# First and second slots staggered per sequence and per expert, features as 128 + 64 on array halves, and the combination joined to the experts

## The chip, the cores and the metric

The kernel runs on one core of a Trainium2 chip. The metric is the device time of one execution in microseconds (us). The core has TensorE (PE; its weight loads are shown as PEld), VectorE (DVE), ScalarE (ACT), GpSimd (POOL) and SyncE (SP, which here only issues transfers). Work on different engines is ordered by semaphores alone. TensorE writes its results to PSUM, which has eight banks of 2 KB in each of 128 partitions.

## What is computed

Eight sequences of 256 tokens with 192 features pass through a token mixer, an attention with 12 heads, and a mixture of experts with two levels of soft slots. The change lies in the last of these. Cut to what matters:

```python
# GROUP = 64 tokens, E1 = 8 outer experts, S1 = 16 slots each, E2 = 4 inner experts each
xn = l2norm(x) * scale * gamma_in ; xg = xn.reshape(b, G, 64, d)         # 32 groups in all
logits1 = einsum('bGgd,esd->bGges', xg, phi)                              # 64 tokens x 128 slots
disp1 = softmax(logits1, axis=2); comb1 = softmax(logits1 over the 128 slots)
slots = einsum('bGgd,bGges->bGesd', xg, disp1)
yn = l2norm(slots) * scale * gamma2
means = yn.reshape(b, G, E1, 4, 4, d).mean(axis=4)
se2 = l2norm(einsum('bGkmd,kdf->bGkmf', means, w_slot2)) * scale          # 192 x 768 weights per k
logits2 = einsum('bGksd,bGkemd->bGksem', yn, se2)
disp2, comb2 = softmax over s, softmax over (e, m)
slots2 = einsum('bGksd,bGksem->bGkemd', yn, disp2)
act = v * gelu(gate), (v, gate) = split(slots2 @ w1 + b1)                 # 32 inner experts
o = act @ w2 + b2
out = einsum(comb1, einsum(o, comb2))                                     # added to the residual h
```

## The kernel before

Everything is float32 outside the attention. A stage is one function with a block of instructions for every engine; between two stages all engines meet. The stages that matter here, in order:

- `fold_weights` (L93) forms, besides the folded weights, the transposed slot table `g.phi_t`, 96 features by two halves by 128 slots.
- `first_slots` (L1181) works on the eight sequences in two rounds of `WIDE` = 4 (a register loop). Within a round every step is done for all four sequences before the next one begins: row statistics, normalized rows `x`, four transposes (L1234), logits to slots and to tokens with the 192 features as 96 + 96 (L1242, L1246), maxima (L1388, L1391), exponentials (L1304, L1308), transposes of both softmax tables (L1253, L1259), the slots (L1267), their squares and norms (L1333, L1415), the means of four slots (L1274, a 128 x 32 stationary matrix) and their transposes (L1280). DVE norms the rows; POOL only clears memory. The dispatch table `disp` has zeros in the rows of the other group, so that each slot product contracts over 128 rows.
- `second_slots` (L1477) makes `se2` for each outer expert k, two buffers in turn in a register loop: a copy of the means (L1596), four products of 384 columns (L1529, 96 + 96 features), squares and root on ACT (L1560 to L1567), scaling on DVE (L1581), eight transposes (L1540) and two copies out, one on DVE and one on ACT (L1590, L1573). SP fetches the weights `w_slot2` of k + 2 when those of k are used (`load_slot2`, L1464).
- `second_dispatch` (L1603) is written out for the eight sequences. PE's order in one iteration n is logits of n (L1649), dispatch turned of n - 1 (L1666), `yn` turned of n + 1 (L1639), logits turned of n (L1658), expert inputs of n - 1 (L1687), weights of n (L1675). The last waits for a product on POOL (L1827), which waits for the row sums of ACT's exponentials (L1724).
- `experts` (L1831) is written out for the 32 inner experts. Its hidden layer already has the features as 128 + 64: whole products (L1882) and then products over 64 rows, alternately in the lower and the upper half of the array (L1887). Each expert's 128 rows are copied from PSUM (L1939), stored to DRAM by ACT's queue (L1919), and once per four experts gathered back into `g.yn` by POOL (L1949), which turns rows of experts into rows of groups.
- `combine` (L1954) adds the bias `b2` to the gathered rows on DVE and POOL (L1980, L1994), copies the mixing weights (L2002), multiplies (L2014), adds the residual (L1984) and stores (L2025).

## Time and profile before

| | us |
|---|---|
| median of three runs | 701.97 |
| lowest and highest | 698.33, 703.11 |
| the profiled execution | 702.88 |
| its span, first to last instruction | 701.1 |
| `first_slots` | 348.5 to 422.7 of the span |
| `second_slots` | 422.7 to 459.9 |
| `second_dispatch` | 459.9 to 532.3 |
| `experts`, its arithmetic | 532.3 to 673.9 |
| gather of the last rows, meeting of the engines | 673.9 to 683.1 |
| `combine` | 683.1 to 701.1 |

The profile is one execution. PE is busy 82% of the span, PEld 67%, DVE 55%, ACT 43%, POOL 10%. Its page shows the granted clock of TensorE in tenths of full speed (2.4 GHz) for 40 slices; the clock has two levels, 1.2 and 2.4 GHz, so that a value of 0.74 means a mixture. A product in float32 has two records in the trace, a transpose has one.

### The profile page before, as it was taken

How to read it: one execution, taken by the hardware profiler on the slowest of the kernel's cores; microseconds unless marked ns; L12 is line 12 of the kernel's file. 1: busy time of each engine (PE TensorE's matmuls, PEld its weight loads, DVE VectorE, ACT ScalarE, POOL GpSimd, SP SyncE). 2: the span in 40 equal slices, each digit the busy share in tenths (PEclk: the TensorE clock that was granted, in tenths of full speed). 3: DMA queues.
4: the chain of work that ended last, by engine and by line, in shares of the span. 5: the costliest groups of instructions: out<-in, count | busy, mean ns of one | idle time of the engine just before them, and what ended most of it. 6: DMA issues, size and time to landing. Idle time of an engine off the chain costs nothing. (4 is left out here: it accounts for less than half of the span.)

```text
span 701.1 us, 12206 instructions
## 1 busy us (share of the span) xinstructions
PE 574.3 (82%) x4294; PEld 469.3 (67%) x4294; DVE 383.4 (55%) x960; ACT 299.5 (43%) x855; POOL 69.8 (10%) x90
## 2 busy tenths in 40 slices
PE   6497997387989989897566877969998999999935
PEld 5386786253666666664365654559987999999934
DVE  2117636658899999986257452435652333333315
ACT  1123432243566566654157775735563222222211
POOL 5682000001000000000000000000000000000004
PEclk9799898665999999999577779968999999999986
DMA  9300000000000000000090003300005999999412
GB/s 320 94 0 2 1 0 1 0 0 1 1 2 2 0 0 0 2 1 1 7 332 0 1 0 93 110 0 1 3 1 216 377 313 322 315 320 284 69 40 91
DMA packets 19656, 58.25 MB, mean 83 GB/s; under 512 B 2627, under 2 KB 9397, under 8 KB 19478
## 3 DMA queue, kind: packets, MB, share of 16 engines
q1 hardware_dynamic: 13366, 47.84, 19.4%
q0 software_dynamic: 1056, 4.73, 3.8%
q10 hardware_dynamic: 5184, 5.02, 2.3%
q8 instruction: 30, 0.49, 0.3%
q14 instruction: 20, 0.16, 0.1%
HBM read 52.86 MB, written 4.72 MB: 82 GB/s over the span
## 5 line engine op out<-in xcount | busy, mean ns | idle before, releaser
L1930 DVE SCALAR_TENSOR_TENSOR ex_act_t<-banks,b_sb,ex_gelu 128x128 f32<-128x128 f32 x128 | 36.1, 345 | 95.6 <-ACT ex_gelu L1913 95.6
L1913 ACT ACTIVATE ex_gelu<-banks,b_sb 128x128 f32<-128x128 f32 x128 | 36.6, 369 | 100.7 <-PE banks L1887 100.7
L1882 PE MATMUL banks<-slots_t,w 128*128 128x128 f32 x512 | 62.5, 275 | 1.0 <-PEq L1606 1.0
L1882 PEld LDWEIGHTS banks<-slots_t,w 128*128 128x128 f32 x512 | 61.2, 192 | 1.4 <-issue 1.3
L1074 DVE TENSOR_REDUCE att_max<-banks 128x4 f32<-128x1024 f32 x48 | 58.6, 1221 | 2.2 <-PE banks L736 1.3
L924 ACT ACTIVATE att_prob<-banks 128x1024 f32<-128x1024 f32 x48 | 49.1, 1023 | 16.6 <-PE banks L759 16.6
L1900 PE MATMUL banks<-w,ex_act_t 128*128 128x192 f32 x256 | 50.2, 339 | 0.6 <-DVE ex_act_t L1930 0.6
L1900 PEld LDWEIGHTS banks<-w,ex_act_t 128*128 128x128 f32 x256 | 40.7, 189 | 4.6 <-DVE ex_act_t L1930 0.9
L1887 PE MATMUL banks<-slots_t,w 64*128 64x128 f32 x512 | 37.2, 285 | 0.0
L736 PE MATMUL banks<-k_t,q_t 96*128 96x256 bf16 x192 | 31.0, 287 | 4.3 <-DVE att_max L1074 4.1
L774 PE MATMUL banks<-att_prob,val 128*32 128x256 f32 x384 | 28.6, 419 | 7.0 <-ACT att_prob L924 6.8
L759 PE MATMUL banks<-q_t,k_t 104*128 104x256 bf16 x192 | 30.7, 284 | 4.0 <-ACT att_prob L924 3.0
L1887 PEld LDWEIGHTS banks<-slots_t,w 64*128 64x128 f32 x512 | 31.1, 187 | 3.9
L709 PE MATMUL banks<-ident_b,att_stack 128*96 128x128 bf16 x384 | 28.4, 231 | 5.2 <-DVE att_stack L1041 2.4
L679 PE MATMUL banks<-qkv_t_sb,xt 96*128 96x384 f32 (+1 forms) x64 | 29.1, 591 | 3.3 <-ACT xt L870 3.3
L709 PEld LDWEIGHTS banks<-ident_b,att_stack 128*96 128x96 bf16 x384 | 26.2, 132 | 7.4 <-DVE q_t L1045 3.5
L899 ACT COPY k_t<-banks 96x1024 bf16<-96x1024 bf16 x24 | 24.1, 1006 | 15.3 <-PE banks L709 15.3
L1166 POOL TENSOR_TENSOR att_qk<-att_qk,qk_weight 128x192 f32<-128x192 f32 x16 | 9.2, 599 | 211.5 <-DVE att_qk L1009 211.5
L1529 PE MATMUL banks<-w_slot,ss_mean_k 96*128 96x384 f32 x64 | 24.0, 524 | 2.9 <-DVE ss_mean_k L1596 2.3
L736 PEld LDWEIGHTS banks<-k_t,q_t 96*128 96x128 bf16 x192 | 15.9, 101 | 13.2 <-DVE att_max L1074 8.6
L759 PEld LDWEIGHTS banks<-q_t,k_t 104*128 104x128 bf16 x192 | 18.1, 100 | 9.8 <-ACT att_prob L924 4.5
L774 PEld LDWEIGHTS banks<-att_prob,val 128*32 128x32 f32 x384 | 10.5, 115 | 19.0 <-ACT att_prob L924 10.6
(231 smaller groups left out, 1171.1 us busy)
## 6 DMA issues: line engine op xcount, KB each, us to landing
w<-in_w SPq DMA_DIRECT2D x32, 768.0 KB, 7.4
w<-in_w2e SPq DMA_DIRECT2D x32, 384.0 KB, 8.1
w_slot<-in_w_slot SPq DMA_DIRECT2D x8, 576.0 KB, 4.5
rows_scratch<-ex_rows ACTq DMA_DIRECT2D x32, 96.0 KB, 6.4
yn_all<-rows_scratch POOLq DMA_DIRECT2D x8, 384.0 KB, 7.2
out<-co_final SPq DMA_DIRECT2D x8, 192.0 KB, 1.9
wk_t<-in_wk_t ACTq DMA_DIRECT2D x1, 579.0 KB, 5.1
wq_t<-in_wq_t SPq DMA_DIRECT2D x1, 579.0 KB, 5.5
```

The costliest lines, as they stand in the source:

```text
L679: last = nc.tensor.matmul(g.ps[banks[1 + t]][:, 0:2 * DIM], x_t[s][0:k, c, t * P:(t + 1) * P], g.t["qkv_t"][0:k, c, 0:2 * DIM], start=(c = ...
L709: last = nc.tensor.transpose(bank[0:KS, h * SEQ + t * P:h * SEQ + (t + 1) * P], stack[:, row, :, :].rearrange("p a b -> p (a b)"), ident_b ...
L736: last = nc.tensor.matmul(g.ps[hh][:, t * SEQ:(t + 1) * SEQ], q_t[s][0:KS, h, t * P:(t + 1) * P], k_t[s][0:KS, h, :], start=True, stop=True)
L759: last = nc.tensor.matmul(g.ps[2 + hh][:, m * SEQ:(m + 1) * SEQ], k_t[s][:, h, m * P:(m + 1) * P], q_t[s][:, h, :], start=True, stop=True)
L774: last = nc.tensor.matmul(bank[32 * j:32 * j + 32, (q % 2) * SEQ:(q % 2 + 1) * SEQ], val[s][:, m, QH * q + j, :], prob[j // 2][:, j % 2, m ...
L924: nc.scalar.activation(prob[u][:, :, :, :].rearrange("p a b n -> p (a b n)"), flat(2, 4), ACT.Exp).then_inc(S["exped"], 1)
L1074: nc.vector.tensor_reduce(neg_max[:, 2 * u:2 * u + 2, :].rearrange("p a b -> p (a b)"), flat(0, 2).rearrange("p (g n) -> p g n", n=SEQ), A ...
L1882: nc.tensor.matmul(bank[:, j * P:(j + 1) * P], g.w1[e][:, first + j * P:first + (j + 1) * P], x[:, 0, :], start=(j == 0), stop=False, skip ...
L1887: last = nc.tensor.matmul(bank[:, j * P:(j + 1) * P], g.w1[e][part, 2 * HID + j * P:2 * HID + (j + 1) * P], x[part, 1, :], start=False, st ...
L1900: last = nc.tensor.matmul(out_bank(n)[:, 0:DIM], act_t[n % 2][:, j * P:(j + 1) * P], g.w2[e][:, j, :], start=(j == 0), stop=(j == HB - 1))
L1913: nc.scalar.activation(gelu[n % 2][:, j * P:(j + 1) * P], gate_bank(n)[:, j * P:(j + 1) * P], ACT.Gelu_apprx_tanh, bias=g.t["b1"][:, n, HB ...
L1930: nc.vector.scalar_tensor_tensor(out=act_t[n % 2][:, j * P:(j + 1) * P], in0=value_bank(n)[:, j * P:(j + 1) * P], scalar=g.t["b1"][:, n, j ...
```

## The change

The arithmetic results stay the same. Four parts:

1. `first_slots` is written out without a loop and staggered: in iteration n each engine works on different steps of sequences n - 3 to n + 1. The features are 128 + 64; sequence tile t has its 64 in the lower (t = 0) or upper (t = 1) half of the partitions. Slots contract over the 64 rows of their group. Normed rows of sequences 1 to 7 and the scaling of the combination table move from DVE to POOL. Slots are normed straight into `g.yn`. The epsilon of the norm comes from a column of 1e-3 beside `x`, so products have 193 columns and two small DVE operations and the accumulation of `disp_sum` fall away. One bank (TURN) takes the turned `x`, dispatch and combination in turn; one pair (SLOTS) takes all slots.
2. `second_slots` is staggered per outer expert, features 128 + 64, three pairs of banks and three weight buffers; the means need no copy; all copies out are on DVE, four per expert.
3. `second_dispatch` reads that layout: six transposes instead of eight, logits as four whole and four half products, expert inputs of the last 64 features alternately in the two column halves. Turned logits and turned dispatch share a bank.
4. `combine` is gone. The experts' stage ends with 32 products of the bias `b2` and 32 products of the gathered rows, accumulated in the eight banks; DVE adds each bank to the residual and SP stores it. The rows of the last four experts go straight from `rows` to `g.yn` by four transfers each, two from SP's queue and two from ACT's; POOL gathers the first seven groups only.

The core of the diff (where an engine's loop calls its steps, the calls stand in order on one or two lines, without their bounds on n and k):

```diff
 def first_slots(nc, g):
+            def logits(n):
+                pe.wait_ge(S["kept"], n + 1)
+                for part in range(2):
+                    for to_slots in (True, False):
+                        for t in range(TPS):
+                            rows, c = chunks(t)[part]     # (0:128, 2t), then (0:64 or 64:128, 1)
+                            last = nc.tensor.matmul(g.ps[LOGITS(n)[t]][:, first:first + P], lhs, rhs,
+                                                    start=(part == 0 and to_slots), stop=(part == 1), ...)
+            def make_slots(n):
+                pe.wait_ge(S["disp_kept"], n + 1)
+                pe.wait_ge(S["slots_normed"], GPS * n)
+                for t in range(TPS):
+                    for half in range(2):
+                        rows = slice(GROUP * half, GROUP * (half + 1))
+                        last = nc.tensor.matmul(g.ps[SLOTS[half]][:, AND_ONE(t)], disp[n % 2][rows, t, :],
+                                                x[n % NX][rows, AND_ONE(t)], start=True, stop=True)
+            # PE
+            for n in range(BATCH + 4):
+                turn_disp(n - 1); logits(n); turn(n + 1); turn_means(n - 3)
+                turn_comb(n - 1); make_slots(n - 1); make_means(n - 2)
+            # ACT
+                squares(n - 2); root_slots(n - 2); keep_mean_rows(n - 3); keep(n + 1); disp_exp(n); comb_exp(n)
+            # DVE
+                keep_disp(n - 1); maxima(n); norm_slots(n - 2); keep_comb(n - 1); keep_means(n - 3)
+                invert(n); row_stats(n + 4)
+            # POOL
+                scale_comb(n); make_x(n + 3)
...
 def second_slots(nc, g):
+            # PE
+            for k in range(E1 + 2):
+                make(k); turn(k - 2)
+            # DVE: norm(k), then keep(k - 1) with four copies of 256 columns. ACT: root(k)
...
 def second_dispatch(nc, g):
-        TURN, LOGITS, TURNED, DISP, WEIGHTS, INPUTS = (0, 1), 2, 3, 4, 5, (6, 7)
+        TURN, LOGITS, SHARED, WEIGHTS, INPUTS = (0, 1), (2, 3), 4, 5, (6, 7)
             def turn_logits(n):
                 pe.wait_ge(S["masked"], n + 1)
-                pe.wait_ge(S["col_exped"], GPS * n)
+                pe.wait_ge(S["disp_kept"], n)
...
 def experts(nc, g):
+            for n in by_bank:                               # (3, 7, 0, 1, 2, 4, 5, 6)
+                mix(n, lambda gr: g.t["b2"], True)
+            pe.wait_ge(gathered, 16 * (E1 - 1))
+            pe.wait_ge(moved, 16 * MEAN * E2)
+            for n in by_bank:
+                mix(n, lambda gr: g.yn[:, n * GPS + gr, :], False).then_inc(S["mixed"], 1)
+        # SP: two transfers of each of the last four experts' rows, then one store per bank
+        # ACT: the other two transfers; DVE: g.h += bank, as mixed counts up
-            for k in range(E1):
+            for k in range(E1 - 1):
...
-def combine(nc, g):
```

## Rows read from the trace of the kernel before

**Rows 1.** Stages: stretch; length, busy PE, PEld, DVE, ACT, POOL, clock, DMA, GB/s.

```profile
348.50:422.70 74.20, 50.87 (x304) 41.64 (x304) 43.01 (x161) 50.24 (x220) 2.46 (x8) 0.74 0.23 80
422.70:459.90 37.20, 31.64 (x128) 19.35 (x128) 14.20 (x24) 21.87 (x88) 0.00 (x0) 0.93 0.34 96
459.90:532.30 72.40, 64.67 (x512) 60.34 (x512) 37.59 (x72) 36.81 (x152) 4.91 (x8) 0.89 0.00 1
532.30:673.90 141.60, 140.45 (x1280) 132.16 (x1280) 44.73 (x160) 37.89 (x129) 3.60 (x7) 1.00 0.86 276
683.10:701.10 18.00, 10.15 (x64) 7.71 (x64) 10.72 (x12) 2.95 (x8) 8.65 (x4) 0.69 0.25 88
```

**Rows 2.** Waits in the first slots: total us, times, longest.

```profile
DVE fs_neg_slot L1388 <- PE banks L1246: 14.3, 8, 4.2
```

**Rows 3.** Timeline in the first slots: start, us, engine, line, what.

```profile
362.51 1.03 PE L1242 MATMUL banks<-fs_x_t,phi_t 96*128 96x256 f32 x4
364.27 1.03 PE L1242 MATMUL banks<-fs_x_t,phi_t 96*128 96x256 f32 x4
...
395.21 0.42 DVE L1388 TENSOR_REDUCE fs_neg_slot<-banks 128x4 f32<-128x256 f32 x1 [4.07 <-PE banks L1246]
...
404.90 6.40 PE L1267 MATMUL banks<-fs_x,fs_disp 128*128 128x192 f32 x32
...
411.47 1.39 DVE L1415 SCALAR_TENSOR_TENSOR fs_yn<-banks,fs_slot_fac,gamma_sb 128x192 f32<-128x192 f32 x4
412.92 0.53 PE L1274 MATMUL banks<-fs_yn,average 128*32 128x192 f32 x8 [1.61 <-DVE fs_yn L1415]
413.47 1.39 DVE L1415 SCALAR_TENSOR_TENSOR fs_yn<-banks,fs_slot_fac,gamma_sb 128x192 f32<-128x192 f32 x4
```

**Rows 4.** Timeline in the second slots.

```profile
443.54 2.75 PE L1529 MATMUL banks<-w_slot,ss_mean_k 96*128 96x384 f32 x8
445.24 0.96 DVE L1581 TENSOR_TENSOR ss_se<-banks,ss_factor 128x768 f32<-128x768 f32 x1 [2.14 <-ACT ss_factor L1567]
446.26 1.08 PE L1540 MATMUL banks<-ident,ss_se 128*96 128x128 f32 x8
447.29 2.85 PE L1529 MATMUL banks<-w_slot,ss_mean_k 96*128 96x384 f32 x8
```

**Rows 5.** Timeline of the second dispatch, and one group of its lines.

```profile
489.44 1.10 PE L1675 MATMUL banks<-comb_t,sd_comb 128*128 128x64 f32 x8 [0.29 <-POOL comb_t L1827]
490.38 2.00 PE L1649 MATMUL banks<-se_t,w_slot 96*128 96x128 f32 x16
496.82 1.10 PE L1675 MATMUL banks<-comb_t,sd_comb 128*128 128x64 f32 x8 [0.28 <-POOL comb_t L1827]
L1687 PE MATMUL banks<-sd_disp,yn_all 128*64 128x128 f32 x16 | 1.6, 279 | 0.0
```

**Rows 6.** Timeline in the experts: whole products, then half products.

```profile
552.96 1.92 PEld L1882 LDWEIGHTS banks<-slots_t,w 128*128 128x128 f32 x16
553.12 1.95 PE L1882 MATMUL banks<-slots_t,w 128*128 128x128 f32 x16
555.00 1.16 PE L1887 MATMUL banks<-slots_t,w 64*128 64x128 f32 x16
```

**Rows 7.** POOL's product with two inputs: a group of the lines.

```profile
L1994 POOL TENSOR_TENSOR co_rows<-yn_all,b_sb 128x768 f32<-128x768 f32 x4 | 8.6, 2181 | 7.0 <-POOLq L1836 6.7 <-PE banks L2014 0.3
```

**Rows 8.** Timeline of the end.

```profile
673.54 0.36 DVE L1939 COPY ex_rows<-banks 128x192 f32<-128x192 f32 x1 [1.39 <-PE banks L1900]
676.09 0.49 POOL L1949 DMA_DIRECT2D yn_all<-rows_scratch  x1 [14.50 <-DMA rows_scratch<-ex_rows]
...
693.31 4.50 PE L2014 MATMUL banks<-co_rows,co_mix 128*64 128x192 f32 x32 [3.12 <-DVE co_rows L1980]
...
697.37 1.23 DVE L1984 TENSOR_TENSOR co_final<-h,banks 128x384 f32<-128x384 f32 x2 [0.72 <-PE banks L2014]
```

**Rows 9.** A stretch of the combination at 1.2 GHz, columns as in the first group.

```profile
683.10:690.00 6.90, 5.46 (x32) 3.70 (x32) 5.01 (x5) 2.54 (x7) 6.75 (x3) 0.50 0.17 59
```

More of the change, by code:

```diff
@@ L42 @@
 BUFS = 8
+SLOT_BUFS = 3
 EARLY = 4
@@ L1347, in _, with keep @@
-            root(0)
-            with act.Fori(0, BATCH // WIDE - 1) as i:
-                body(i, more=True)
-            body(BATCH // WIDE - 1, more=False)
+                act.wait_ge(S["logged"], pair + 1)
+                nc.scalar.activation(factor[:, cols], log_v[:, cols], ACT.Exp, scale=-0.5).then_inc(S["rooted"], 1)
+            def keep(n):
+                act.wait_ge(S["turned"], n + 1)
+                if n >= 2:
+                    act.wait_ge(S["logits"], n - 1)
+                nc.scalar.copy(x_t[n % 2][:, :, :], g.ps[TURN][:, 0:3 * P].rearrange("p (c n) -> p c n", c=3)
+                               ).then_inc(S["kept"], 1)
@@ new lines, in _ @@
+            root(0)
+            keep(0)
+            root(1)
+            for n in range(BATCH + 4):
+                if 0 <= n - 2 < BATCH:
+                    squares(n - 2)
+                    root_slots(n - 2)
+                if 0 <= n - 3 < BATCH:
+                    keep_mean_rows(n - 3)
+                if n + 1 < BATCH:
+                    keep(n + 1)
+                if n < BATCH:
+                    disp_exp(n)
+                    comb_exp(n)
+                if n in (1, 3):
+                    root(2 + n // 2)
@@ new lines, in _ @@
+            for n in range(2):
+                row_stats(n)
+            make_x(0)
+            for n in range(2, 4):
+                row_stats(n)
+            for n in range(BATCH + 4):
+                if 0 <= n - 1 < BATCH:
+                    keep_disp(n - 1)
+                if n < BATCH:
+                    maxima(n)
+                if 0 <= n - 2 < BATCH:
+                    norm_slots(n - 2)
+                if 0 <= n - 1 < BATCH:
+                    keep_comb(n - 1)
+                if 0 <= n - 3 < BATCH:
+                    keep_means(n - 3)
+                if n < BATCH:
+                    invert(n)
+                if n + 4 < BATCH:
+                    row_stats(n + 4)
@@ L1577, in _, with norm @@
+                nc.scalar.activation(log_s[:, k, :], ss[:, k, :], ACT.Ln, scale=1.0 / DIM,
+                                     bias=g.eps_dim[:, :]).then_inc(S["logged"], 1)
+                act.wait_ge(S["logged"], k + 1)
+                nc.scalar.activation(factor[:, k, :], log_s[:, k, :], ACT.Exp, scale=-0.5).then_inc(S["rooted"], 1)
+            for k in range(E1):
+                root(k)
         @block.vector
         def _(dve):
-            def norm(i, s):
-                dve.wait_ge(S["rooted"][s], i + 1)
+            def norm(k):
+                dve.wait_ge(S["rooted"], k + 1)
+                if k >= 2:
+                    dve.wait_ge(S["turned"], k - 1)
@@ L1603, in second_dispatch @@
+            for k in range(E1 + 1):
+                if k < E1:
+                    norm(k)
+                if k >= 1:
+                    keep(k - 1)
 def second_dispatch(nc, g):
```

803 lines of the change are left out of this document (376 added, 427 removed).

## Prediction

> **What bounds the kernel now.** I first cut the span into its stages, since a share of busy time over the whole span says little [rows 1]. In the experts PE is busy 140.45 of 141.60 us at full clock. The change leaves their arithmetic alone, so those 141.6 us stay. In the first slots no engine is full: PE 50.9, ACT 50.2 and DVE 43.0 of 74.2 us, and the clock is 0.74. The waits say why: each step is done for four sequences while the other engines stand, for instance DVE waits 14.3 us in all for logits [rows 2]. In the second slots PE is busy 31.6 of 37.2 us, in the second dispatch 64.7 of 72.4 us, so there PE's own work counts. The timeline of the end shows a stretch without arithmetic: the last expert's rows are copied at 673.54 to 673.90, the gather is issued at 676.09, and the combination begins at 683.1 and takes 18.0 us with PE busy 10.2 [rows 1, 8]. From the last copy to the end are 27.2 us.
>
> **Prices.** A whole product of 128 columns costs 0.122 us per record (1.95 / 16). Over 64 rows in alternate array halves it costs 0.073 (1.16 / 16), a factor of 0.6 [rows 6]. A transpose costs 0.135 (1.08 / 8) [rows 4]. A change between whole and half products leaves PEld idle for 555.00 - (552.96 + 1.92) = 0.12 us, while the PE records leave no gap [rows 6]. So such a switch costs between 0 and 0.12 us; I take 0.12, as weight loads set this pace. The Trainium skill, "TensorEngine Tiling (Array Packing)", Key Properties, says that changing the tiling mode drains the engine, and gives no figure for it. By that rule the 0.12 is a drain, and by the PE records alone it would be free; what each makes of the first slots stands below, in its own bounds.
>
> **First slots.** The loop that closes from one iteration to the next runs PE, DVE, PE, because make_slots(n - 1) has to wait until norm_slots(n - 2) has read the only pair of slot banks, and DVE puts maxima(n) ahead of that norm. Its terms:
> - two transposes of the dispatch, 0.27;
> - logits, 8 whole records at 0.122 and 8 half ones at 0.073: 1.56 (now 1.76, from 362.51 to 364.27 [rows 3]);
> - two maxima of 256 columns, 2 x 0.42 = 0.84;
> - norm of four slots, 1.39 (rows of 192 columns);
> - slots, 8 half records of 193 columns: 6.40 / 32 = 0.20 whole, times 0.6 = 0.12, so 0.96;
> - means, 0.53;
> - five hand-overs between engines, as an estimate 0.3 in all (two of them, 0.04 us each: DVE's reduction starts as PE's records end);
> - four more switches, 0.5.
>
> That is 6.35 us per sequence at 2.4 GHz [rows 3, 6]. 3.3 us of it is PE work, which at 1.2 GHz nearly doubles. What clock will be granted? The stage has 0.74 now, about half its time at the lower level. The staggered PE has gaps of about 1 us and work in about 4.3 of 6.35 us, denser than now (50.9 of 74.2 includes the wait for the half clock itself). I take a quarter of the time at the lower level: 6.35 + 0.8, so 7.1. Six iterations take 43 us. The first two have no norm on the path: 3.75 each, 7.5. Ahead lie statistics, root, one normed sequence, transposes and copy, 5 us. At the end nothing overlaps: norm of 6, slots of 7, squares and root (2.0, the distance of two norms on rows 3, and 0.4 for the wait), norm, means, their copies and transposes: 10.8. The sum is 66, against 74.2: **-8**. Bounds: all at 2.4 GHz and switches free, 5.85 per iteration, gives 58 (-16); a clock of 0.74 as now and every switch paid gives 8.0 per iteration and 73 (-1). Other engines lie beside this loop. ACT has now 50.2 / 8 = 6.3 us per sequence and loses the 32 accumulator reads of the dispatch and the copy into `g.yn`, so about 5. DVE has 0.4 + 0.84 + 1.39 + 0.4 + three copies of the means 0.8 + statistics 0.9, about 5. POOL is new here. Its row is 2.18 us for 768 columns with two inputs, taken in proportion: 0.73 for the table of 256 and 1.09 + 2 x 0.55 for one normed sequence, 2.9 in all; the bounds are 0.6 times that (one input) and a fixed part that doubles it to 5.8, still under the loop [rows 7].
>
> **Second slots.** Now 447.29 - 443.54 = 3.75 us per expert [rows 4]. After: four whole records of 384 columns at 2.75 / 8 = 0.344, four half at 0.6 of it, 2.2 us; transposes 0.98; two switches 0.24: 3.4. Seven times 0.35 saves 2.4, the copy of the means ahead of the first product 0.5. But DVE now takes all copies, four of about 0.38 after the 0.96 of the scaling, and with one pair of TURN banks the last transposes wait for them: two rounds of transposes and copies (5 us) now follow one another where one and a half did, +2. Together **-1**, between -4 (switches free, tail as now) and +2.
>
> **Second dispatch.** The period is 496.82 - 489.44 = 7.38 us [rows 5]. PE gets shorter by 2 transposes (0.25), logits 1.79 to 1.56 (0.23), and the 16 records over 64 columns (1.6 us) at about 0.6 of that, 0.6. It would save 1.0 less 0.24 for two switches. But the chain logits, mask, row maximum, exponentials, reciprocal, POOL, weights is already the last to arrive (PE waits 0.28 for POOL), and it gets shorter only by the logits and by an earlier turned `yn`, 0.4 to 0.5. The shared bank makes turn_logits(n) wait for ACT's copy of the dispatch; behind it on PE stand the inputs and weights. The copy is ready about 0.15 us late, which the same chain hides. **-3.5** for eight iterations, from 0 to -7.
>
> **End.** Removed: store, gather, meeting of engines, bias additions, copies of the mixing weights. Added: 64 records of 192 columns for the bias on PE, right after the last expert. At 1.2 GHz such a record takes 5.46 / 32 = 0.17 us [rows 9]; at a mixed clock 4.50 / 32 = 0.14 [rows 8]. After the experts the clock is 1.00 [rows 1], so between 0.085 (half) and 0.14; I take 0.10. PE: 673.5 + 6.4 + 6.4 = 686.3, then as now from the last product (697.8) to the end, 3.3: 689.6, **-11.5**. Bounds: 0.085, -13.5; 0.17 throughout, -2.5. The four last transfers are issued from 673.9, two on each queue, behind nothing but each other (SP's weight loads are long done), and the bias products cover them until 679.9. Without that cover they would cost their issue and landing, some 3 us. The store now lands within 676.09 - 673.9 = 2.2 us [rows 8].
>
> **Sum.** -8 - 1 - 3.5 - 11.5 = -24. Against the profiled execution, 702.88 us (0.9 above the median), this gives 679, and 678 by the median; I state **679**.
>
> **Rivals.**
> - *A, the clock stays at 1.2 GHz in the three stages* (the other side). For it: the clock is 0.74 in the first slots now, and spreading the work leaves a gap of about 1 us in each iteration. Against: 0.93 and 0.89 in the second slots and the second dispatch, where PE also waits in every iteration [rows 1, 5]. Price: first slots 6.35 + 3.0 = 9.3 per iteration, 81 in all (+7); second slots 3.4 to about 4.9 (+8); second dispatch, PE's 6 us to 11 per iteration, 88 against 72.4, +16; end -11.5: together +20, **722**. It ends slower once more than about half of the three stages runs at the lower level. The Trainium skill, "TensorE: Matmul & The Clock Gate", Part 4: PE-mode transpose, says that transposes do not count as activity for the clock; by that rule a third of the staggered PE work would not help to hold it. Chance 0.06.
> - *B, the first slots gain nothing*: the loop is 8 us or more, because POOL's rows of `x` or the half products are dearer than taken. Time 702.9 - 16 = **687**. For it: POOL's price is taken from another operation. Chance 0.16.
> - *C, the end gains little*: the mixing products run at 0.17, or the last transfers land after the bias products. 27.2 - 2.5 of it stays: **688**. Against: 1.00 right before. Chance 0.10.
> - *D, all at 2.4 GHz and switches free*: -16 - 3 - 6 - 13.5, **664**. Chance 0.13.
> - *Forecast*, 671 to 686: 0.55.
>
> **How the numbers follow.** The range takes in D's end, B and C: 664 to 692, and leaves out A and mixtures of B and C. Over 1% (7 us, about what a measurement of this kernel can tell) faster are forecast, B, C and D but for 0.05 where B and C come together: 0.89. Within 1%: 0.05. Slower: 0.06.
>
> **What would show it.** In the profile after: the first slots in 66 us with make_slots at a distance of about 7.1 and released by DVE's norm; a clock over 0.8 there; half products at 0.6 of whole ones; second slots about 36 us; second dispatch about 69; no gap over 0.5 us on PE between the last expert and the last mixing product, and 16 us from the last copy to the end. I am wrong if PE waits for POOL in the first slots, if the clock there is under 0.7, or if the final products wait for a transfer.

## The result, and the profile after

| | before | after |
|---|---|---|
| median of the runs, us | 700.7 (698.33 to 703.11) | 672.65 (668.68 to 672.94) |
| span of the profiled execution, us | 701.1 | 671.0 |
| mean granted clock | 0.883 | 0.898 |

The ratio is 0.9586, with a 95% interval of 0.9535 to 0.9638: 4.1% faster. The forecast was 679 with a range of 664 to 692. Direction and range held. The two profiled executions differ by 29.9 us and the medians by 28, where 24 were forecast, so I look at each stage.

The same cut into stages for the kernel after, to be read beside [rows 1]. I put the borders at the end of the last attention addition, the first product of the second slots, the first transposes of the second dispatch, the first product of the experts, and the end of the last copy of rows. Columns: stretch, length, busy PE, PEld, DVE, ACT, POOL, clock, DMA share, GB/s.

```profile
347.33:410.32 62.99, 40.52 (x328) 28.24 (x329) 37.28 (x131) 33.71 (x168) 26.21 (x37) 0.85 0.27 104
410.32:446.15 35.83, 29.60 (x128) 16.48 (x129) 21.20 (x40) 14.88 (x80) 0.00 (x0) 0.83 0.25 83
446.15:514.90 68.75, 59.41 (x497) 51.86 (x497) 36.87 (x72) 36.03 (x153) 4.91 (x8) 0.88 0.00 1
514.90:655.95 141.05, 140.85 (x1286) 132.55 (x1288) 44.60 (x160) 37.84 (x129) 3.58 (x7) 1.00 0.87 276
655.95:671.00 15.05, 10.37 (x126) 9.19 (x122) 4.44 (x8) 0.00 (x0) 0.00 (x0) 0.98 0.35 115
```

With the same borders the kernel before has 74.66, 36.90, 72.42, 141.42 and 27.20 us, after 348.50 us of embedding, mixer and attention (347.33 in the kernel after). So:

| stage | before | after | change | forecast |
|---|---|---|---|---|
| first slots | 74.66 | 62.99 | -11.7 | -8 |
| second slots | 36.90 | 35.83 | -1.1 | -1 |
| second dispatch | 72.42 | 68.75 | -3.7 | -3.5 |
| experts | 141.42 | 141.05 | -0.4 | 0 |
| end | 27.20 | 15.05 | -12.15 | -11.5 |

These give -28.9. Another 1.2 lies ahead of the first slots, in code that is the same in both but for the layout of the transposed slot table. That part moves by itself: in the profiles of this study the attention ends between 347.2 and 349.9 us, whatever the kernel. I therefore compare **spans less the end of the attention**: 352.6 for before, 323.7 for after. For a kernel that was profiled twice (after, and after once more) this number is 323.67 and 323.70, where the spans differ by 2.6.

**The loop of the first slots.** One iteration in the timeline of the kernel after (start, us, engine, line, what, and in brackets the idle time ahead and what ended it). It answers [rows 3].

```profile
380.76 0.44 PE L1276 MATMUL banks<-ident,fs_disp_t 128*128 128x128 f32 x2
381.04 0.61 PE L1258 MATMUL banks<-fs_x_t,phi_t 128*128 128x128 f32 x4
381.72 0.21 ACT L1374 ACTIVATE fs_slot_fac<-fs_slot_log 128x4 f32<-128x4 f32 x1
382.35 0.39 PE L1258 MATMUL banks<-phi_t,fs_x_t 64*128 64x128 f32 x4
382.79 0.42 DVE L1412 TENSOR_REDUCE fs_neg_slot<-banks 128x4 f32<-128x256 f32 x1 [1.12 <-PE banks L1258]
383.46 1.38 DVE L1436 SCALAR_TENSOR_TENSOR yn_all<-banks,fs_slot_fac,gamma_sb 128x192 f32<-128x192 f32 x4
...
384.76 0.41 DVE L1423 COPY comb_t<-banks 128x256 f32<-128x256 f32 x1
384.99 0.93 PE L1286 MATMUL banks<-fs_x,fs_disp 64*128 64x193 f32 x8 [0.75 <-DVE yn_all L1436]
385.09 0.93 DVE L1444 COPY means_t<-banks 128x128 f32<-128x128 f32 x3
386.16 0.53 PE L1295 MATMUL banks<-yn_all,average 128*32 128x192 f32 x8 [0.25 <-DVE means_t L1444]
386.63 0.44 PE L1276 MATMUL banks<-ident,fs_disp_t 128*128 128x128 f32 x2
```

Up to the slots the chain runs as the forecast drew it: transposes, logits, DVE's maxima, DVE's norm, slots (released by that norm). From 380.76 to 386.63 one iteration takes 5.87 us. Its pieces are 1.98 + 0.05 for transposes and logits, 0.67 for the maxima, 1.38 + 0.15 for the norm, 1.17 for the slots and 0.47 for the means. The 1.17 are 0.93 of products and then a wait that the forecast did not have: the means of one sequence go to the bank from which DVE copies the turned means of the one before, and DVE comes to these three copies only behind the norm and the copy of the combination table. They end at 386.02, TensorE's slot products about 0.1 us earlier, and the means begin at 386.16. The distance of the slot products is 5.86 to 5.87 us each time from the third of them to the seventh.

And the clock, over three stretches of that stage:

```profile
347.33:360.00 12.67, 6.61 (x40) 5.39 (x40) 6.23 (x27) 3.49 (x14) 7.23 (x16) 0.64 0.92 351
360.00:400.00 40.00, 28.77 (x262) 20.43 (x259) 25.94 (x89) 27.92 (x142) 18.99 (x22) 1.00 0.13 53
400.00:410.32 10.32, 5.14 (x32) 2.42 (x31) 5.11 (x17) 2.30 (x12) 0.00 (x0) 0.54 0.01 2
```

In the loop it is 1.00, so 2.4 GHz throughout. It is low at the start, where TensorE waits for statistics and the first features, and in the drain.

Between whole and half products the weight loads leave a gap:

```profile
381.37 0.53 PEld L1258 LDWEIGHTS banks<-phi_t,fs_x_t 128*128 128x128 f32 x4
382.02 0.30 PEld L1258 LDWEIGHTS banks<-fs_x_t,phi_t 64*128 64x128 f32 x4
```

**POOL.** From the groups of lines of the stage (count, busy us, mean ns, idle before):

```profile
L1499 POOL TENSOR_SCALAR fs_centred<-h,fs_mv,fs_factor 128x192 f32<-128x192 f32 x14 | 14.0, 1009 | 5.0 <-DVE fs_x L1457 3.4 <-ACT fs_factor L1334 1.6
L1505 POOL TENSOR_TENSOR fs_x<-fs_centred,gamma_in_sb 128x384 f32<-128x384 f32 x7 | 7.0, 1003 | 0.6
```

A sequence costs 2 x 1.01 + 1.00 and 0.61 for the table, 3.6 us.

**Second slots and second dispatch.** Timeline of TensorE at their border, to be read beside [rows 4, 5]:

```profile
438.21 1.75 PE L1587 MATMUL banks<-ident,ss_se 128*128 128x128 f32 x8 [1.97 <-DVE se_t L1635]
441.92 1.94 PE L1587 MATMUL banks<-ident,ss_se 128*128 128x128 f32 x8 [1.97 <-DVE se_t L1635]
...
455.67 1.97 PE L1726 MATMUL banks<-comb_t,sd_comb 128*128 128x64 f32 x8 [2.60 <-POOL comb_t L1883]
...
465.72 1.10 PE L1726 MATMUL banks<-comb_t,sd_comb 128*128 128x64 f32 x8 [0.66 <-POOL comb_t L1883]
...
472.68 0.55 PE L1726 MATMUL banks<-comb_t,sd_comb 128*128 128x64 f32 x3 [0.36 <-POOL comb_t L1883]
```

The last two rounds of transposes run one behind the other with DVE's copies and TensorE idles 1.97 us ahead of each. The clock is at its lower level from 438.4 to 452.1 us and again from 455.5 to 462.3, and the first period of the dispatch is long: 465.72 - 455.67 = 10.05 us, where the next is 472.68 - 465.72 = 6.96. Another 9.5 us lie ahead of the first of these products.

**The end**, beside [rows 8]:

```profile
655.48 5.42 PE L1980 MATMUL banks<-b_sb,mix_t 128*64 128x192 f32 x64
655.59 0.36 DVE L2037 COPY ex_rows<-banks 128x192 f32<-128x192 f32 x1 [1.40 <-PE banks L1972]
662.66 5.42 PE L1980 MATMUL banks<-yn_all,mix_t 128*64 128x192 f32 x64 [1.76 <-DMA yn_all<-ex_rows]
663.57 5.11 DVE L2043 TENSOR_TENSOR h<-h,banks 128x384 f32<-128x384 f32 x8 [7.62 <-PE banks L1980]
```

Each mixing record takes 5.42 / 64 = 0.085 us, and there is a wait that the forecast did not have: 1.76 us for the last transfers.

### The profile page after: what moved, and what is told of

Its sections match the earlier page's. It is cut to its first block and busy times, and to the rows that moved or that the text cites. A ratio compares the mean times of both kernels' runs of the same rounds, so it can differ in the third digit from the quotient of the medians.

```text
span 671.0 us, 12001 instructions
## 1 busy us (share of the span) xinstructions
PE 558.5 (83%) x4367; PEld 447.4 (67%) x4367; DVE 377.9 (56%) x944; ACT 272.0 (41%) x787; POOL 84.4 (13%) x114
## 5 line engine op out<-in xcount | busy, mean ns | idle before, releaser
L777 PE MATMUL banks<-att_prob,val 128*32 128x256 f32 x384 | 30.0, 437 | 7.0 <-ACT att_prob L927 6.8
L739 PEld LDWEIGHTS banks<-k_t,q_t 96*128 96x128 bf16 x192 | 15.9, 101 | 13.5 <-DVE att_max L1077 8.6
L1099 DVE COPY q_t<-banks 8x1024 bf16<-8x1024 bf16 x24 | 16.7, 697 | 12.0 <-PE banks L749 11.3
```

The source lines that it names most:

```text
L739: last = nc.tensor.matmul(g.ps[hh][:, t * SEQ:(t + 1) * SEQ], q_t[s][0:KS, h, t * P:(t + 1) * P], k_t[s][0:KS, h, :], start=True, stop=True)
L777: last = nc.tensor.matmul(bank[32 * j:32 * j + 32, (q % 2) * SEQ:(q % 2 + 1) * SEQ], val[s][:, m, QH * q + j, :], prob[j // 2][:, j % 2, m ...
```

## The experiments

All ratios are to the kernel before, measured beside each run. "Less the attention" is the profiled span less the end of the attention.

### One part alone

`tail_only` is the kernel before with the new end: `experts` as after, no `combine`.

```diff
-        experts(nc, g)
-        combine(nc, g)
+        experts(nc, g)
...
+            for n in by_bank:
+                mix(n, lambda gr: g.yn[:, n * GPS + gr, :], False).then_inc(S["mixed"], 1)
```

> The kernel before with the new end alone: experts with the joined combination, all stages ahead of them as before. Theory (the parts add up, each worth what its stretch shortened): from the last copy of rows to the end 15 us instead of 27.2, so about 12 us less than before, 688.5, ratio 0.983. Rival (part of the 28 us comes from the parts together, such as a cooler start of the experts or freed buffers): less than 10 us gained, or the other parts together gain less than 16.

Measured: 690.29 us, ratio 0.984 (0.9811 to 0.9868), less the attention 342.5 against 352.6. The end took 14.97 us against 27.20, a gain of 12.2. The whole gained 10.1: the first slots took 76.02 and the second slots 37.75 in this run, 1.4 and 0.85 more than before, with not a line of them changed. In the first slots 0.9 of the 1.4 came at the start: the granted clock rose to its upper level 12.5 us after the attention, and 10.6 us after it in before. Where the low stretches fall shifts by itself and moves stages by 1 to 2 us, so a single stage's total is no finer than that.

`first_only` is the kernel before with the new first slots; the means are handed on as 96 + 96, as the old second slots want them.

```diff
+                for c in range(2):
+                    nc.vector.tensor_copy(
+                        g.means_t[:, c, :, n * GPS:(n + 1) * GPS, :],
+                        g.ps[MEANS][0:HALF, 2 * P + c * P:2 * P + (c + 1) * P].rearrange(
+                            "p (g k m) -> p k g m", g=GPS, k=E1)).then_inc(S["means_kept"], 1)
```

> The kernel before with the new first slots alone (staggered, 128 + 64, rows of x on POOL); only the turned means are still kept as 96 + 96, for the unchanged second slots. Theory: the stage shortens from 74.7 to about 63 us, as in the changed kernel, so 11 to 12 us less than before, 689, ratio 0.984. Rival (the gain in the stage is partly paid by the next one, whose products start at 1.2 GHz): 6 to 9 us.

Measured: 689.78 us, ratio 0.9833 (0.9805 to 0.9862), less the attention 339.8, a gain of 12.8. The first slots took 61.3 us, 1.7 less than in after, and the distance of the slot products in the loop was 5.55 us where it is 5.87 in after. The two kernels differ in these steps by the copies of the turned means, two here and three in after:

```profile
385.36 0.93 PE L1285 MATMUL banks<-fs_x,fs_disp 64*128 64x193 f32 x8 [0.75 <-DVE yn_all L1435]
385.46 0.47 DVE L1442 COPY means_t<-banks 96x128 f32<-96x128 f32 x2
386.22 0.53 PE L1294 MATMUL banks<-yn_all,average 128*32 128x192 f32 x8
```

The two copies take 0.47 us where the three take 0.93, and TensorE no longer waits ahead of the means. So in after the copies behind DVE's norm are part of the loop, and the third one costs 0.3 us per sequence.

`no_tail` is the kernel after with the old end, so it has the second slots and second dispatch on top of `first_only`.

```diff
         experts(nc, g)
+        combine(nc, g)
```

> The kernel after with the end of the kernel before: experts without rows moved as they come, and a combination of its own; first slots, second slots and second dispatch as in after. Against the kernel before with the new first slots alone (span 688.1) it has the second slots and the second dispatch beside it. Theory (the stretches of the profile add up): those two give 1.1 + 3.7 us, so the span is 683 to 684 and the ratio about 0.976. Rival (what the runs with one part left over, 701 to 672.65 less 10.5 and 11.0, belongs to these two): 6.6 us, span 681.5 and ratio 0.973. Against after (671.0) it should be slower by the 10.5 to 12 us of the end.

Measured: 685.08 us, ratio 0.9779 (0.9749 to 0.9809). Second slots 35.84, second dispatch 68.79 us, as in after. Less the attention it is 336.7: 3.1 under `first_only` and 13.0 over after. By the ratios that is 0.0054 of 701, 3.8 us. These 3.1 us are not all that the two middle stages bring: `no_tail` has the third copy of the means, and its first slots took 63.1 us, 1.8 more than in `first_only`. In their own stretches the second slots gained 1.2 and the second dispatch 4.1. The end brought 12.2 us in its stretch in `tail_only` and 12.9 here (27.9 and 15.0). On the whole it was 10.1 there and 13.0 here, and 2.2 of this difference are the two slot stages of `tail_only` told of above. By stretches the parts add up within the 1 to 2 us above.

### Features of 96 + 96 in the first slots

`whole_feats` is the kernel after with turned features and logits of the first slots as two chunks of 96, so 16 whole records in place of 8 whole and 8 half ones, and four transposes in place of three.

```diff
-                for part in range(2):
+                for c in range(2):
                     for to_slots in (True, False):
                         for t in range(TPS):
-                            rows, c = chunks(t)[part]
-                            of_x, of_phi = x_t[n % 2][rows, c, :], g.phi_t[rows, c, :]
+                            of_x, of_phi = x_t[n % 2][:, c, t * P:(t + 1) * P], g.phi_t[:, c, :]
```

> The changed kernel with the features of the first slots as 96 + 96 again: four transposes and eight products over 96 rows per sequence instead of three and four whole plus four half ones; staggering and slots over 64 rows as changed. Theory (staggering makes the gain of the stage, halves only shorten logits on the loop by 0.2 to 0.4 us per sequence): the distance of two slot products goes from 5.86 to 6.1 to 6.3 us, the kernel 2 to 3 us slower than the changed one, 675. Rival (halves carry the gain): 6 us slower or more. Second rival (switches eat what halves save): within 1 us.

Measured: 677.05 us, ratio 0.9642 (0.9604 to 0.968), span +4.8, less the attention 328.1, +4.4. The result lies between the two: more than the 2 to 3 us of the theory, less than the 6 of the rival. The first slots took 68.9 us, 5.9 more than in after. At 2.4 GHz the distance of the slot products is 6.10, that is +0.24 per iteration, near the 0.2 that the forecast gave the logits. Most of the rest is the clock. The start runs at 1.2 GHz until 15.9 us after the attention, where it was 9.2 in after, and the longer products fall into it:

```profile
354.52 1.06 PE L1257 MATMUL banks<-phi_t,fs_x_t 96*128 96x128 f32 x4
...
365.23 0.93 PE L1285 MATMUL banks<-fs_x,fs_disp 64*128 64x193 f32 x8
```

The first slot product comes 17.6 us after the attention, where after needs 361.75 - 347.33 = 14.4. One distance of 7.74 us inside the loop, with a clock of 0.83 from 385 to 395 us, adds 1.6. The second dispatch was 1.3 shorter than in after, without an edit.

### The norm ahead of the maxima

In the loop DVE does the maxima of sequence n ahead of the norm of n - 2, and TensorE waits for that norm. `norm_first` swaps the two.

```diff
-                if n < BATCH:
-                    maxima(n)
                 if 0 <= n - 2 < BATCH:
                     norm_slots(n - 2)
+                if n < BATCH:
+                    maxima(n)
```

> The changed kernel with one swap on DVE in the first slots: the norm of slots n - 2 ahead of the maxima of n. Theory (the loop PE, DVE, PE through the single pair of slot banks sets the pace, and the order on DVE puts maxima on it): slots are released about 1.5 us earlier, the distance of two slot products falls from 5.86 to about 5.0 us, where ACT (about 4.7 us of work) comes near, and the kernel is 4 to 6 us faster than the changed one, 667. Rival (another chain, ACT's or POOL's rows of x, is as long): 5.7 us or more, within 1 us.

Measured: 673.2 us, ratio 0.9602 (0.9576 to 0.9629), less the attention 323.5 against 323.7. My theory fell. The equal total hides a loss: the first slots took 64.05 us, 1.1 more than in after, and the second slots 34.58, 1.25 less at a clock of 0.89 for 0.83, with no edit of theirs. The timeline of the first slots:

```profile
374.11 0.93 ACT L1349 ACTIVATE fs_disp_t<-banks,fs_neg_slot 128x64 f32<-128x64 f32 x4 [1.35 <-DVE fs_neg_tok L1414]
...
375.40 0.53 PE L1295 MATMUL banks<-yn_all,average 128*32 128x192 f32 x8 [0.91 <-DVE means_t L1444]
...
377.21 0.32 ACT L1366 ACTIVATE fs_square<-banks 128x193 f32<-128x193 f32 x1
...
378.82 0.20 ACT L1374 ACTIVATE fs_slot_fac<-fs_slot_log 128x4 f32<-128x4 f32 x1
...
379.06 1.39 DVE L1436 SCALAR_TENSOR_TENSOR yn_all<-banks,fs_slot_fac,gamma_sb 128x192 f32<-128x192 f32 x4 [1.87 <-ACT fs_slot_fac L1374]
...
380.60 1.50 PE L1286 MATMUL banks<-fs_x,fs_disp 64*128 64x193 f32 x8 [0.47 <-DVE yn_all L1436]
```

In after ScalarE has the slot factors ready at 381.93, and the norm begins only at 383.46, behind the maxima. That 1.5 us the swap was to free. In this iteration of `norm_first` the factors came late instead, and DVE stood idle 1.87 us for them. The chain behind it: the maxima come late, now between the norm and the copies of the means, so TensorE waits 0.91 us for these copies where it waited 0.25. ScalarE's exponentials come late too, and in ScalarE's queue the squares of the next norm stand behind those, and here also behind a wait of 1.03 us for DVE's row statistics. They begin 2.7 us after the slot products end, where in after they follow at once. The loop is a ring over three engines, and a place gained for one step was taken from another on the same ring. Two distances grew to 7.0 and 6.5 us, two others fell to 5.4 and 4.5. The clock was 0.83 from 376 to 386 us here, so part of the 6.5 can be the clock's.

### The features on DVE

`x_on_dve` makes the normed features of sequences 1 to 7 on DVE instead of POOL.

```diff
                 if n + 4 < BATCH:
                     row_stats(n + 4)
+                if n + 3 < BATCH:
+                    make_later_x(n + 3)
...
                 scale_comb(n)
-                if n + 3 < BATCH:
-                    make_x(n + 3)
```

> The kernel after with the normed features of the first slots (two subtract-multiply and one multiply per sequence) made on DVE, behind the norm of the third sequence back, in place of POOL; nothing else differs. Theory (the first slots are bound by the chain through DVE, and POOL's 3.6 us per sequence lie beside it): the two 192-column operations and one of 384 columns cost DVE about 1 us per sequence and what it was doing comes later, so the distance of the slot products grows from 5.86 to 6.5 to 7.5 us and the span by 4 to 10 us. Rival (DVE has that much slack inside the loop): distance within 0.2 us of 5.86 and the span within 2 us of 671; moving the work to POOL then was worth nothing.

Measured: 673.67 us, ratio 0.9597 (0.9549 to 0.9645), less the attention 323.2: no difference in the whole. But the first slots took 65.25 us, 2.3 more. The first slot product came 1.1 us later after the attention. Of the next three distances two were longer, 6.63 and 6.33 against 5.96 and 5.86; from then on they are 5.86. The clock was 0.74 over the first of these and 1.00 over the other, so the clock has no part in the 0.47 of the other, and may have one in the 0.67. The three operations cost DVE 0.67 + 0.56 us, under half of POOL's 3.0:

```profile
371.77 0.64 DVE L1468 TENSOR_SCALAR fs_centred<-h,fs_mv,fs_factor 128x192 f32<-128x192 f32 x2
372.45 0.56 DVE L1474 TENSOR_TENSOR fs_x<-fs_centred,gamma_in_sb 128x384 f32<-128x384 f32 x1
```

The 2.3 us came back in the second dispatch, 66.0 us in place of 68.75, in a stage that is the same instruction for instruction. Its first period took 8.55 us in place of 10.05, and its last 8 us ran at a granted clock of 1.00, and at 0.79 in the kernel after, which was worth 1.6. So moving the features was right by at most 2.3 us in its stage, less than my 4 to 10 (of which the clock's share is not separated), and this gain is smaller than what the clock gives and takes elsewhere.

### The clock in the drains

`filled` puts 71 products that nobody reads where TensorE would stand idle or thin: at the end of the first slots, at the end of the second slots, in the first iteration of the second dispatch.

```diff
+            def fill(count):
+                for _ in range(count):
+                    nc.tensor.matmul(g.ps[1][:, 0:P], g.ident[:, :], g.ident[:, :], start=True, stop=True)
...
+                if n == BATCH + 1:
+                    fill(9)
                 if 0 <= n - 2 < BATCH:
                     make_means(n - 2)
+                if n == BATCH:
+                    fill(7)
```

> The kernel after with 71 more products whose result nobody reads (128 x 128 of the fp32 identity, into a bank that is free then), placed where TensorE idles and its clock falls: 31 in the last two and a half iterations of the first slots, 28 in the last two transposes of the second slots and behind them, 12 in the first iteration of the second dispatch. What the reference asks for is computed unchanged. Theory (the low clock in these places costs time): the granted clock stays near 1.0 from 400 to 466 us in place of 0.54, 0.83 and 0.68. The two dispatch iterations of 9.1 us come to 7.0 (-4.2), the last two transposes of the second slots from 1.75 and 1.94 us to half (-1.8, less the idle time that grows), the first experts of the second slots -1: span 663 to 666, ratio to the kernel before about 0.947. Rival (these stretches wait for DVE and ScalarE, whose work does not depend on the clock): the products run faster and the waits grow by as much, and some filling products delay the work behind them: span 670 to 675, ratio 0.956 to 0.965.

Measured: 662.97 us, ratio 0.9429 (0.938 to 0.9478), less the attention 314.7, 9.0 under after. The same stages:

```profile
347.88:411.15 63.27, 45.45 (x390) 34.60 (x391) 37.29 (x131) 33.62 (x168) 26.19 (x37) 0.93 0.27 104
411.15:444.24 33.09, 32.26 (x184) 20.94 (x185) 21.20 (x40) 14.85 (x80) 0.00 (x0) 1.00 0.28 91
444.24:506.19 61.95, 55.41 (x520) 48.21 (x521) 36.75 (x72) 36.08 (x153) 4.90 (x8) 1.00 0.00 1
```

The clock is 1.00 in the second slots and the second dispatch. The first slots gain nothing (+0.3); the second slots gain 2.7, of which 2.0 in their first expert, and the second dispatch 6.8: 5.2 in its first two iterations, and the rest at its end, which now stays at full clock without any filling of its own. The wait for the last transfers is still there, 1.67 us.

`filled_start` fills the start of the first slots too.

```diff
+            fill(14, 6)
             turn(0)
+            fill(3, 6)
             for n in range(BATCH + 4):
+                if n == 1:
+                    fill(7, 0)
```

> The kernel with filling products (span 662.6) with 24 more at the start of the first slots, where TensorE waits for the first features and the first exponentials and its granted clock was 0.64 from 347 to 360 us, and three fewer at the end of the first slots, where the last eight ended 0.3 us before the second slots could begin. The output is computed unchanged. Theory (the low clock costs time here too): the first logits and transposes, 3.7 us of products at the low clock, take 2 us; the first slot product starts at 360 in place of 362.3 and the span is 660 to 661, about 2 us under the version before it. Rival (the first two sequences wait for the statistics, POOL's features and ScalarE's exponentials): the first slot product at 362 and the span 662 to 663.

Measured: 665.16 us, ratio 0.9505 (0.948 to 0.953), less the attention 314.1. The first 14 products ran at 1.2 GHz and were still running when the first features were ready:

```profile
348.42 5.84 PE L1308 MATMUL banks<-ident 128*128 128x128 f32 x28 [1.28 <-POOL fs_x L1537]
354.09 0.49 PE L1243 MATMUL banks<-ident,fs_x 128*128 128x128 f32 x3
```

They held the first transposes back, and the higher clock behind them gave as much back: the first slot product came 14.7 us after the attention, against 14.4 in after. The rival held. The ratio is higher than that of `filled`, and the median by 2.2 us, but on another chip and against another set of runs of before, while the profile less the attention is 0.6 lower. Between these two kernels nothing is shown.

`filled_less` leaves those 14 out, and ran beside the kernel after.

> The kernel after once more, unchanged, beside the filled version on one chip. All theories: 671 to 673 us and a ratio to the kernel before of 0.956 to 0.961.

> The kernel with filling products at the start too, without the 14 ahead of the first transposes, which held these back from 351.4 to 354.1 us; three behind them, seven ahead of the first turned exponentials and five (not eight) at the end of the first slots stay. Theory (filling pays where TensorE's own products come behind it at once, and costs where it delays one): first slot product at 361 to 362, span 660.5 to 662, 9 to 11 us under after measured beside it (ratio to the kernel before about 0.944). Rival (the gain of the filled version over after was partly one of chips or of runs): less than 6 us under after.

Measured side by side: after 673.61 us (0.9561, 0.9517 to 0.9605), the filled kernel 664.98 us (0.9435, 0.9386 to 0.9484), so 8.6 less. Less the attention: 323.7 and 313.8. So the gain of 9 to 10 us belongs to the filling and not to a difference between chips. Its span, 663.7 us, is higher than I expected because the attention ended at 349.90 us in both. At the start the three and seven products brought no more than 0.2 us: the first slots took 62.85 us against 63.02, and the first slot product came no earlier.

### What the last transfers wait for

`no_bias` leaves the 64 bias products out, and with them the bias `b2`.

```diff
-            for n in by_bank:
...
-                mix(n, lambda gr: g.t["b2"], True)
+            pe.wait_ge(S["gelued"], HB * N)
+            pe.wait_ge(S["acted"], HB * N)
+            pe.wait_ge(S["kept"], N)
```

> The kernel after without the 64 bias products of the second combination (the second bias b2 is left out of the output); the mixing products of the experts' rows open their banks instead. Theory (the bias products are hidden behind the landing of the last rows, and the last transfers, not TensorE, set when the mixing begins): TensorE idles about 7.2 us (5.4 + 1.8) for the transfers ahead of the mixing, which begins within 0.5 us of where it did, and the span changes by less than 1 us. Rival (the bias products cost time of their own, or the landing depends on what TensorE does): the mixing begins 2 to 5 us earlier. A third possibility: the idle 7 us let the clock fall, and the mixing products take up to 0.17 us each where they took 0.085, so the span grows by 2 to 5 us.

`one_move` moves each of the last four experts' rows with one transfer from SP in place of four from two queues.

```diff
-                move_rows(sp, n, range(0, MEAN // 2))
+                sp.dma_start(g.yn[n * MEAN:(n + 1) * MEAN, :, :],
+                             rows[n % ROWS][:, :]).then_inc(moved, 16)
```

> The kernel after with each expert's rows (four partitions, for the last experts issued by SP and ScalarE, two partitions each) moved in one transfer issued by SP. Theory (the landing of 5.5 to 6.0 us is mostly the writing of four partitions of 24 KB, whoever issues): a single transfer lands in about the same time, the wait of TensorE ahead of the mixing stays at 1 to 3 us, and the span within 1.5 us. Rival (most of the landing is a cost of each issue, one after the other on its queue): one transfer lands 1.5 us earlier or more, the wait of 1.76 us goes, and the span falls by 1 to 2 us.

Measured: `no_bias` 676.97 us, ratio 0.9617 (0.9557 to 0.9677); `one_move` 676.76 us, 0.9616 (0.9559 to 0.9673); less the attention 325.9 and 326.2 against 323.7. TensorE's timeline, `no_bias` first:

```profile
656.30 1.57 PE L1972 MATMUL banks<-w,ex_act_t 128*128 128x192 f32 x8 [0.20 <-DVE ex_act_t L2020]
665.02 7.59 PE L1980 MATMUL banks<-yn_all,mix_t 128*64 128x192 f32 x64 [7.16 <-DMA yn_all<-ex_rows]
```

```profile
658.28 5.42 PE L1981 MATMUL banks<-b_sb,mix_t 128*64 128x192 f32 x64
666.06 7.10 PE L1981 MATMUL banks<-yn_all,mix_t 128*64 128x192 f32 x64 [2.35 <-DMA yn_all<-ex_rows]
```

Without the bias products TensorE waits 7.16 us in place of 5.42 + 1.76 = 7.18. From the end of the last copy of rows to the first mixing product it is 6.76 us in `no_bias` and 662.66 - 655.95 = 6.71 in after. So the transfers alone set when the mixing begins; the bias products are hidden and cost nothing. More than that, they pay: after 7 us of standing the mixing took 7.59 us and not 5.42, since the clock fell, and the end grew by 2.2 us (17.24). The third possibility of the expectation came true.

One transfer is no better. In the chain of what ended last, the last transfer took 6.00 us in after and 7.15 here:

```profile
658.78 7.15 DMA yn_all<-ex_rows
```

The wait grew to 2.35, the clock fell there too, and the end took 17.25 us. From the last copy to the first mixing product it is 7.3 us in place of 6.7. So four transfers from two queues were ready 0.6 us sooner than one transfer from one queue; whether the number of transfers or that of the queues does it is not separated. The rival, a cost of each issue, did not come true: with one issue in place of four the landing did not get shorter. The traces show two things about the rest. Between 657 and 661 us of the kernel after the rows moved at 29 GB/s; at this rate the 98 KB of the last expert alone take 3.4 us, an estimate. And four transfers of an expert that met less of the others' (issued from 650.4 us) took 3.8 to 4.3 us to land, where the last four, issued while four others were in flight, took 5.5 to 6.0. What sets the rate stays open.

## Why the prediction was right or wrong

**First slots (forecast -8, measured -11.7 in the stage; `first_only`, whose loop is 0.3 us shorter, gains 12.8).** The staggering works as forecast, and DVE's norm ends the wait of the slot products. The loop was priced at 6.35 us at 2.4 GHz and takes 5.86. The maxima advance in 0.67 and not 0.84, since the second starts before the first one's duration is over. TensorE's own work in the chain takes 1.98 + 0.93 + 0.47 = 3.38, against 3.82 with the switches and 3.32 without: nearly all of the 0.5 for switches was not paid, though the weight loads show a gap at the switch to half products, 382.02 - (381.37 + 0.53) = 0.12 us. One term was missing: 0.24 us for DVE's copies behind the norm, which the forecast counted only among DVE's work beside the loop. `first_only`, with one copy less, shows it by 5.55 for 5.87. So that the loop met the bound of 5.85 is in part luck: free switches and shorter maxima less a wait that the bound did not have. The larger error is the quarter of the time at the lower clock, 0.8 us per iteration: in the loop it was none. I had read the clock of a stage whose work stands in clumps, 0.74 [rows 1], as a property of the stage. Against that the two ends were too cheap: 15.3 us to the second turned dispatch (362.61) against 12.5, and 12.0 for the drain against 10.8, both at a low clock. Six iterations make -7.2, the ends +4.0: 63.0 in place of 66.

The Trainium skill, "TensorE: Matmul & The Clock Gate", Part 4: PE-mode transpose, says that transposes do not count as busy in the same way as products. Here 1.6 of TensorE's 4.5 busy us per iteration were transposes and the clock stayed at 1.00. No run separates the rule itself, but it would have spoken for rival A, and A did not come.

**POOL** was priced from an operation of another kind at 2.9 us, with 5.8 as the upper bound; it took 3.6. The single-input operation on 192 columns is the term that was off, 1.01 us for 0.55. It did not matter for the path, as the forecast said.

**Second slots (-1, measured -1.1).** The period is 3.16 us per expert where 3.4 was forecast: the whole records are 1.46 / 4 = 0.365 and the half ones 0.92 / 4 = 0.23, but neither switch appears in the sum. From the first expert's products to the eighth's it is now 22.6 us where it was 28.0, a gain of 5.4 where 2.4 were forecast. From the eighth's products to the second dispatch it is 13.2 where it was 8.9, a loss of 4.35 where 2 were forecast. So the sum is right by two errors that cancel. The first expert ran at the low clock, which cost 2.0 us as `filled` shows and was not in the sum; the kernel before has a low stretch at its start too.

**Second dispatch (-3.5, measured -3.7).** Here too the sum is right by errors that cancel. The period is 6.96, 0.42 shorter, as the shorter chain through POOL promised, and from the second weights to the last, six periods, it is -2.4. The start up to the second weights is 2.4 us shorter where two periods would give 0.8, and the last stretch, behind the last weights, is 1.1 us longer. The low clock costs 5.2 us in the first two iterations and 1.6 at the end, as `filled` shows; before had its low stretches at the start alone (0.89 over the stage [rows 1]), and how much they cost there is not tried. Whether the shared bank costs anything is not tried.

**End (-11.5, measured -12.15).** Two terms were off, in opposite directions, and a small one: what follows the mixing took 2.9 us for 3.3. The mixing records took 0.085 and not 0.10, which is 1.9 us less over 128 records. The step "the bias products cover the transfers until 679.9" failed: I gave issue and landing "some 3 us" with a store to memory as the only row [rows 8], and from the last copy to the first mixing product it is 6.7 us. The cover is 1.76 us short. My own sign of error, the final products waiting for a transfer, appeared, and it cost less than rival C's 9.

**The rivals.** A did not come: the loop held the full clock. B did not come. C's condition did, transfers that land after the bias products, but it cost 1.76 us and not 9. D (664) had the length of the loop and the mixing right, but not the ends of the stage. Its sum takes -3 and -6 for the two middle stages, where the bounds worked out for them were -4 and -7; with these it would be 662. The time lies near the lower edge of the forecast's own 671 to 686.

## What to carry to other kernels

The staggered stage kept its clock in the loop here and lost it at its ends. Inside the loop it was not safe either: in `whole_feats`, `norm_first` and `x_on_dve` the clock fell once there. Price the fill and the drain of each stage by themselves, at 1.2 GHz, and add what the next stage's first instructions lose. List in the chain of a loop also the work that the engine does behind the step that you look at, where another step waits for it: one copy of 0.3 us on DVE was 0.3 us of the loop. Where TensorE stands at such an end, products that nobody reads bought 9 us of 673 here, and the same kind of product, placed where the next real one has to queue behind it, bought nothing. Before two steps in an engine's queue are swapped to shorten one wait, follow the ring through all engines: the step that moves back may stand on the same ring.

## What the runs showed of the hardware

- The last expert's four transfers from the rows in SBUF to one partition each of another tile (24 KB each, on two queues) took 5.5 to 6.0 us from issue to landing, and one transfer of all four partitions 7.15. The Trainium skill, "DMA: Bandwidth & Descriptors", Anatomy of one DMA, gives about 2.0 us plus bytes / 436e9 for a DMA issued by POOL; by that figure 98 KB would take 2.2 us, an estimate. These, issued by SP and ScalarE, took far longer, so the page's figure does not carry over to them.
- POOL took 1.01 us for one-input work on 192 columns, 1.00 us for two-input work on 384 and 0.61 on 256, where DVE took 0.67 for two of the first and 0.56 for the second. The operation with scalars from two columns was the dear one per column on POOL.
- The granted clock was 1.00 in a loop of 5.86 us in which TensorE had two or three gaps of 0.25 to 0.75 us, while it fell right behind a wait of 1.97 us at the end of the second slots, in a wait of 2.60 us in the second dispatch, and in the wait of 7.16 us in `no_bias`. It did not fall with the wait of 1.76 us at the end. 71 added products raised the mean clock of the execution from 0.898 to 0.928. The Trainium skill, "TensorE: Matmul & The Clock Gate", Part 1: The HAM clock gate, says that the throttled state is the default and activity releases it; by that rule added products should raise it, and the trace agrees.
